# Finishing stage of a two-layer transformer taken into the coupling stage: turn back, residual, normalise and store, two tiles at a time, a thousand tokens behind

## The chip, the cores and the metric

The kernel runs on one core of a Trainium2 chip, as one launch. The metric is the device time of that core in microseconds (us). The kernel before took 5580.25 us, the median of three runs (5573.52 to 5586.86).

## What is computed

Two post-norm layers over 4096 tokens of 256 features, all in float32. Each layer is an attention block and a feed-forward block, and behind each block the residual is added and the row normalised. The change touches only the last block, the "coupling" network of the second layer, and the last normalisation. Cut to what matters:

```python
def _L1_ffn_ref(x, ...):
    gf = _global_net(x.mean(axis=1, keepdims=True), ...)      # one number for the sequence
    out = x
    for _ in range(3):
        # tf: 256 -> 256 -> 128 -> 64 -> 1 with gelu between, sigmoid at the end, one number per token
        tf = _coupling_net(out, cn_w1, cn_b1, ..., cn_w4, cn_b4)
        combined = 0.7 * gf + 0.3 * tf
        coupling = 0.1 + adaptive_range * (combined - 0.5) * 2.0
        out = out + coupling * _twist(out)                    # _twist swaps the halves with signs
    return out

x = _layernorm(x + _L1_ffn_ref(x, ...), axis=-1)              # the last line of the reference
```

So each token goes three times through a small network, which changes it; then its old value is added, its 256 features are normalised, and the row is stored.

## The kernel before

The kernel is a chain of stages: `project` and `attention` for layer 0, `mlp_weights` and `mlp`, `project` and `attention` for layer 1, `mix_out`, `coupling`, `finish`. Between two stages stand `core.clear()`, which frees the semaphores, and a barrier of all engines. Within a stage every engine has its own instruction stream, in the order in which the code is written, and waits on semaphores (`wait_ge`) that the others raise (`then_inc`). No scheduler moves anything.

Names: a tile is 128 tokens (P), there are 32 (NT). A block is 512 tokens (QB), there are 8 (N). `x_all` (in `build` it is `a_all`) holds the layer's input with tokens on partitions, `xT_all` the same values with features on partitions, in two chunks c of 128 features. `ps` is the accumulator memory with eight banks of 512 floats.

`coupling` works on pairs of blocks: a loop `r` over 4 pairs, in it 3 cycles `cyc`, in it both blocks `q` of the pair, layer by layer. TensorE computes layer 1 for both blocks (L1541, banks 2q and 2q+1), then layer 2 (L1549, bank 4+q), then layers 3 and 4 (L1554 and L1557, both in bank 6+q). ScalarE follows with gelu, gelu, gelu and tanh (L1578 and L1579, L1583, L1587, L1591). VectorE then makes the coefficient (L1506), two products (L1510, L1511), and changes `xT_all` in place (L1513, L1514); the last raises `x_new[q]`. In cycles 1 and 2 layer 1 of a block waits for `x_new[q]`; in cycle 0 it doesn't, since the next pair of blocks is independent of the last. TensorE, ScalarE and VectorE each run the loop with a hardware counter (`Fori`) and take addresses and wait values from registers. A float32 matmul stands in the trace as two MATMUL records.

`finish` then goes over the 32 tiles, one at a time. TensorE turns a tile of `xT_all` back with two transposes (L1610). VectorE adds the old value (L1640), takes the statistics (L1645, L1647), adds epsilon (L1649); GpSimd raises to the power -0.5 (L1622); VectorE normalises (L1631); SyncE's queue stores the tile (L1656). In VectorE's order the normalisation of tile i-1 stands behind the addition of tile i and ahead of its statistics.

## Time and profile before

| | |
|---|---|
| median of three runs | 5580.25 us (5573.52 to 5586.86) |
| the profiled execution's own time | 5566.02 us |
| its span | 5564.2 us |
| TensorE busy | 5047.7 us, 91% |
| VectorE busy | 4709.1 us, 85% |
| ScalarE busy | 3734.5 us, 67% |
| GpSimd busy | 218.6 us, 4% |

Most of the span is attention, in two stretches with all three compute engines busy. The two stages of this change are the last 292 us: `coupling` computes from 5272.0 us on, its last write is done at 5500.1 us, and `finish` takes the rest. Times are us from the start of the span. An entry "[3.16 <-DVE xT_all L1514]" says that the engine was idle for 3.16 us before the row and that this instruction ended it; "PE" is TensorE's matmuls, "PEld" its weight loads, DVE is VectorE, ACT ScalarE, POOL GpSimd, SP SyncE. A row with "xN" merges N instructions and its time runs from the start of the first to the end of the last. "PEclk" is the clock granted to TensorE, 1.00 for 2.4 GHz and 0.50 for 1.2 GHz.

### The profile page before, as it was taken

What the parts mean: (1) busy time and instruction counts of PE and PEld (TensorE: products, weight loads), DVE (VectorE), ACT (ScalarE), POOL (GpSimd) and SP (SyncE); (2) the same over time, 40 slices, a digit from 0 to 9 for tenths busy, and PEclk for the clock granted to TensorE, in tenths of its full rate; (3) what the DMA queues carried; (4) which work ended last, traced back from release to release, by engine and by line L of the source; (5) the groups of instructions that cost most, each with busy time, mean ns of one, the idle gap of its engine ahead of it and who ended that gap; (6) DMA issues with size and microseconds to landing.
All of it is one profiled execution on the core that took longest, in us unless ns stands there. A gap on an engine that the chain in (4) does not pass through costs nothing. (4 is left out here: it accounts for less than half of the span.)

```text
span 5564.2 us, 124831 instructions
## 1 busy us (share of the span) xinstructions
PE 5047.7 (91%) x43370; PEld 2092.7 (38%) x43370; DVE 4709.1 (85%) x5375; ACT 3734.5 (67%) x7102; POOL 218.6 (4%) x278
## 2 busy tenths in 40 slices
PE   7599999999999588767999999999999999999686
PEld 4233434433444255432333333333333333333332
DVE  3588889889888689739999999999999999999535
ACT  2068787787777311123888888888888888888331
POOL 3100000000000000030000000000000000000201
PEclk7589999999999799986999999999999999999886
DMA  4301010010010100060100001000100001000000
GB/s 125 102 18 31 14 35 15 11 41 8 11 41 11 27 11 12 17 204 12 41 8 5 5 18 31 5 5 8 38 8 8 5 5 41 8 5 5 8 0 30
DMA packets 152926, 142.93 MB, mean 26 GB/s; under 512 B 72490, under 2 KB 107242, under 8 KB 152298
## 3 DMA queue, kind: packets, MB, share of 16 engines
q1 hardware_dynamic: 152330, 134.93, 8.6%
q8 instruction: 380, 6.23, 0.5%
q14 instruction: 216, 1.77, 0.1%
HBM read 86.84 MB, written 46.66 MB: 24 GB/s over the span
## 5 line engine op out<-in xcount | busy, mean ns | idle before, releaser
L926 DVE TENSOR_REDUCE att_mx<-ps 128x2 f32<-128x1024 f32 (+2 forms) x3335 | 3899.7, 1193 | 284.9 <-PE ps L801 208.5
L907 ACT ACTIVATE att_probs<-ps 128x512 f32<-128x512 f32 (+3 forms) x6400 | 3388.7, 583 | 644.1 <-PE ps L843 202.0
L870 PE MATMUL ps<-att_probs,att_V 128*17 128x256 f32 (+1 forms) x25088 | 1950.0, 385 | 0.0
L843 PE MATMUL ps<-att_Q,K 50*128 50x512 f32 (+3 forms) x6400 | 1675.8, 491 | 44.6 <-ACT att_probs L907 24.8
L801 PE MATMUL ps<-K,att_Q 48*128 48x512 f32 x6670 | 1460.0, 419 | 140.2 <-DMA K<-khi_scratch 81.7
L843 PEld LDWEIGHTS ps<-att_Q,K 50*128 50x128 f32 x6400 | 649.9, 184 | 1383.1 <-ACT att_probs L907 1314.8
L870 PEld LDWEIGHTS ps<-att_probs,att_V 128*17 128x17 f32 x25088 | 426.7, 96 | 1054.5 <-issue 590.3
L801 PEld LDWEIGHTS ps<-K,att_Q 48*128 48x128 f32 x6670 | 668.2, 192 | 229.0 <-DVE att_mx L926 138.0
L887 ACT ACTIVATE att_negT<-ps 32x128 fp32r<-32x128 f32 x66 | 16.6, 252 | 231.9 <-PE ps L811 231.9
L1181 PE MATMUL ps<-wguT,mlp_xqT 128*128 128x512 f32 (+1 forms) x384 | 163.4, 577 | 0.5 <-DVE mlp_h L1284 0.2
L791 PE MATMUL ps<-att_band,att_pick 64*128 64x128 bf16 x2080 | 162.9, 224 | 0.0
L1506 DVE TENSOR_SCALAR cn_cf<-cn_th,cn_ab 128x512 f32<-128x512 f32 x24 | 13.0, 544 | 151.5 <-ACT cn_th L1591 151.5
L1541 PE MATMUL ps<-xT_all,cn_w 128*128 x192 | 109.9, 737 | 27.7 <-DVE xT_all L1514 25.8
L1220 ACT ACTIVATE mlp_gate<-ps 128x704 f32<-128x704 f32 x32 | 24.2, 758 | 144.3 <-PE ps L1181 139.4
L1226 ACT ACTIVATE mlp_hqT<-ps 128x640 f32<-128x640 f32 x32 | 22.5, 703 | 132.6 <-PE ps L1190 132.6
L483 DVE TENSOR_TENSOR proj_qprod<-ps,proj_tabT 128x1024 f32<-128x1024 f32 x32 | 38.4, 1220 | 82.0 <-PE ps L329 82.0
L1362 POOL MEMSET mix_power<- 128x1 f32 x1 | 0.1, 98 | 2697.8 <-POOLq L131 2697.8
L1181 PEld LDWEIGHTS ps<-wguT,mlp_xqT 128*128 128x128 f32 x384 | 74.4, 201 | 74.6 <-issue 66.2
L1199 PE MATMUL ps<-wdT,mlp_hqT 128*128 128x256 f32 (+1 forms) x384 | 95.3, 391 | 1.1 <-DVE mlp_y L1258 1.1
L392 ACT ACTIVATE proj_xT<-ps 128x512 f32<-128x512 f32 x32 | 17.5, 595 | 117.2 <-PE ps L311 117.2
L1578 ACT ACTIVATE cn_h<-ps,cn_b 128x512 f32<-128x512 f32 x24 | 16.5, 687 | 114.4 <-PE ps L1541 114.4
L791 PEld LDWEIGHTS ps<-att_band,att_pick 64*128 64x128 bf16 x2080 | 67.9, 96 | 50.6 <-issue 26.6
(211 smaller groups left out, 2424.6 us busy)
## 6 DMA issues: line engine op xcount, KB each, us to landing
K<-khi_scratch SPq DMA_DIRECT2D x320, 64.0 KB, 2.3
att_Q<-qhi_scratch SPq DMA_DIRECT2D x272, 64.0 KB, 2.3
att_V<-v_scratch SPq DMA_DIRECT2D x80, 136.0 KB, 2.5
K<-klo_scratch SPq DMA_DIRECT2D x160, 64.0 KB, 2.3
v_scratch<-proj_vpad SPq DMA_DIRECT2D x16, 544.0 KB, 3.4
att_Q<-qlo_scratch SPq DMA_DIRECT2D x136, 64.0 KB, 2.3
att_Q<-att_negT SPq DMA_DIRECT2D x264, 4.0 KB
proj_x<-in_L_attn_x SPq DMA_DIRECT2D x8, 512.0 KB, 5.4
```

Source lines behind the costliest of these rows:

```text
L483: dve.tensor_tensor(prod[name][:, m], of[name], tabT[:, j % 2, m, :].unsqueeze(1).to_broadcast([P, 2, B]), ALU.mult).then_inc(prods[name], 1)
L791: return pe.matmul(dst, pick[rows, m], band[rows, m, kind], start=False, stop=(m == 1))
L801: mm = pe.matmul(bank(b)[:, 0:wide], Q[rows, slot_of(u), j, qt * P:(qt + 1) * P], K[rows, u // NQB, j, c * QB:c * QB + wide], start=True, ...
L843: mm = pe.matmul(ring(at)[:, lo:QB], K[rows, u // NQB, j, kt * P:(kt + 1) * P], Q[rows, slot_of(u), j, lo:QB], start=True, stop=not diagonal)
L870: mm = pe.matmul(ps[VW * h:VW * h + HV, 6, lo:(part + 1) * (QB // 2)], V[:, v // NQB, kt, HV * h:HV * (h + 1)], probs[:, (n_key[v] + kt) % ...
L907: act.activation(probs[:, (n_key[u] + kt) % PBUFS, column(h), lo:QB], ring(at)[:, lo:QB], ACT.Exp, scale=SCALE).then_inc(emptied, 1)
L926: dve.tensor_reduce(mx[:, min(u % NQB, 1), :, j, qt, c], ps[:, 2 + 2 * pair:4 + 2 * pair, 0:max_width(u, i) // 2], AX.X, ALU.max).then_inc ...
L1181: mm = pe.matmul(gu_ps[:, b:to], xqT[:, par, c, :], wguT[:, c, b:to], start=(c == 0), stop=(c == DC - 1))
L1199: mm = pe.matmul(down, hqT[0:kw, par, k, :], wdT[0:kw, k, :], start=(k == 0), stop=(k == NK - 1))
L1220: act.activation(gate[:], gate_ps, ACT.Silu).then_inc(s["gate_kept"], 1)
L1226: act.activation(hqT[:, par, 0:full], hqT_ps[:, 0:full], ACT.Copy).then_inc(s["hq_kept"], 1)
L1541: mm = pe.matmul(ps[:, 2 * q + m, :], w1[:, c, m * P:(m + 1) * P], xT_all[:, c, bass.ds(r * (2 * QB) + q * QB, QB)], start=(c == 0), stop= ...
```

## The change

`finish` as a stage of its own is gone, with the clear and barrier before it. Its work is in `coupling`, on pairs of tiles (256 tokens, 16 pairs p, four to each r):

- TensorE turns pair p back with four transposes into bank 6 + p % 2. While loop r works on its 1024 tokens, the four pairs of r-1 are turned back, behind layer 1 of both blocks and ahead of layer 2: two pairs in cycle 0, one each in cycles 1 and 2. The last four pairs come after the loop.
- VectorE settles a pair (addition over 512 columns, two normalisations of the pair before, two of each statistics instruction, one epsilon) at four places, `hosts`: in cycle 0 behind block 0 and behind block 1, in cycles 1 and 2 behind block 1. The last four pairs, and the last normalisation, come after the loop.
- GpSimd takes one power per pair, SyncE stores one pair (256 KB) per DMA, 16 instead of 32.
- Banks 6 and 7 are given to the pairs, so layer 3 goes to bank 2q and layer 4 to bank 4+q. Layer 1 now also waits for the gelu that read layer 3 of the cycle before, layer 2 for the tanh of the cycle before.
- The loops over r are written out instead of counted by hardware, on all engines.

```diff
@@ -1408,7 +1408,7 @@
                         steps.end()
 
 
-def coupling(nc, core, ps, w, xT_all, sums):
+def coupling(nc, core, ps, ident, w, xT_all, sums, x_all, out):
 
 
     CYCLES = 3
@@ -1444,7 +1444,15 @@
         coef = core.pair("cn_coef")
         twisted = core.pair("cn_twisted")
         x_new = core.pair("cn_x_new")
+        y, z = sb("y", [P, 2, 2, D]), sb("z", [P, 2, 2, D])
+        st, mv = sb("st", [P, 2, 6]), sb("mv", [P, 2, 2, 2])
+        var, rstd, power = sb("var", [P, 2, 2]), sb("rstd", [P, 2, 2]), sb("power", [P, 2])
+        f = {n: core.sem("cn_" + n) for n in ("turned", "ln_steps", "root", "normed")}
+        stored = core.pair("cn_stored")
         NETS = 13
+        PAIR_STEPS = 6
+        PAIRS_R = 2 * QB // (2 * P)
+        hosts = {(0, 0): 0, (0, 1): 1, (1, 1): 2, (2, 1): 3}
         with nc.Block() as block:
             @block.sync
             def _(sp):
@@ -1460,6 +1468,12 @@
+                for p in range(NT // 2):
+                    sp.wait_ge(f["normed"], 2 * p + 2)
+                    sp.dma_start(out[2 * p * P:(2 * p + 2) * P, :].rearrange("(g p) d -> p g d", p=P), z[:, p % 2]
+                                 ).then_inc(stored[p % 2], 16)
+                for par in range(2):
+                    sp.wait_ge(stored[par], 16 * (NT // 4))
 
             @block.gpsimd
             def _(pool):
@@ -1468,6 +1482,14 @@
                 pool.memset(sign[P // 2:P], -1.0).then_inc(s["set"], 1)
+                pool.wait_ge(s["set"], 3)
+                pool.memset(power[:], -0.5).then_inc(s["set"], 1)
+                pool.wait_ge(s["set"], 4)
+                for p in range(NT // 2):
+                    pool.wait_ge(f["ln_steps"], (p + 1) * PAIR_STEPS)
+                    if p >= 2:
+                        pool.wait_ge(f["normed"], 2 * (p - 1))
+                    pool.tensor_tensor(rstd[:, p % 2], var[:, p % 2], power[:], ALU.pow).then_inc(f["root"], 1)
 
             @block.vector
             def _(dve):
@@ -1496,12 +1518,40 @@
 
                 for q in range(2):
                     dve.sem_inc(coef[q], 1)
-                with dve.Fori(0, N // 2) as r:
+
+                def norm(p):
+                    dve.wait_ge(f["root"], p + 1)
+                    if p >= 2:
+                        dve.wait_ge(stored[p % 2], 16 * (p // 2))
+                    for t in range(2):
+                        dve.tensor_scalar(z[:, p % 2, t], y[:, p % 2, t], mv[:, p % 2, t, 0:1], rstd[:, p % 2, t:t + 1],
+                                          ALU.subtract, ALU.mult).then_inc(f["normed"], 1)
+
+                def settle(p):
+                    steps = Chain(dve, f["ln_steps"], p, PAIR_STEPS)
+                    dve.wait_ge(f["turned"], p + 1)
+                    if p >= 2:
+                        dve.wait_ge(f["normed"], 2 * (p - 1))
+                    steps.put(dve.tensor_tensor(y[:, p % 2], ps[:, 6 + p % 2, :].rearrange("p (t d) -> p t d", t=2),
+                                                x_all[:, 2 * p:2 * p + 2, :], ALU.add))
+                    if p >= 1:
+                        norm(p - 1)
+                    steps.ready()
+                    for t in range(2):
+                        steps.put(dve.bn_stats(st[:, t], y[:, p % 2, t]))
+                    steps.ready()
+                    for t in range(2):
+                        steps.put(dve.bn_aggr(mv[:, p % 2, t], st[:, t]))
+                    steps.ready()
+                    steps.put(dve.tensor_scalar(var[:, p % 2], mv[:, p % 2, :, 1], EPS, None, ALU.add))
+                    steps.end()
+
+                for r in range(N // 2):
                     for cyc in range(CYCLES):
                         for q in range(2):
                             at = r * CYCLES + cyc
-                            a = xT_all[:, 0, bass.ds(r * (2 * QB) + q * QB, QB)]
-                            b = xT_all[:, 1, bass.ds(r * (2 * QB) + q * QB, QB)]
+                            a = xT_all[:, 0, (2 * r + q) * QB:(2 * r + q + 1) * QB]
+                            b = xT_all[:, 1, (2 * r + q) * QB:(2 * r + q + 1) * QB]
                             dve.wait_ge(act_done[3][q], at + 2)
                             dve.tensor_scalar(cf[:, q], th[:, q], ab[:, 4:5], ab[:, 5:6], ALU.mult, ALU.add
                                               ).then_inc(coef[q], 1)
@@ -1512,6 +1562,11 @@
                             dve.wait_ge(twisted[q], at + 1)
                             dve.tensor_tensor(a, a, turn[:, q, 0], ALU.add)
                             dve.tensor_tensor(b, b, turn[:, q, 1], ALU.subtract).then_inc(x_new[q], 1)
+                            if r >= 1 and (cyc, q) in hosts:
+                                settle((r - 1) * PAIRS_R + hosts[cyc, q])
+                for p in range(NT // 2 - PAIRS_R, NT // 2):
+                    settle(p)
+                norm(NT // 2 - 1)
 
             @block.tensor
             def _(pe):
@@ -1528,7 +1583,19 @@
                 for n in range(4):
                     for q in range(2):
                         pe.sem_inc(mm_done[n][q], 1)
-                with pe.Fori(0, N // 2) as r:
+
+                def turn_back(p):
+                    r, q = p // PAIRS_R, p % PAIRS_R // 2
+                    pe.wait_ge(x_new[q], (r + 1) * CYCLES)
+                    if p >= 2:
+                        pe.wait_ge(f["ln_steps"], (p - 2) * PAIR_STEPS + 1)
+                    for t in range(2):
+                        for c in range(DC):
+                            mm = pe.transpose(ps[:, 6 + p % 2, (t * DC + c) * P:(t * DC + c + 1) * P],
+                                              xT_all[:, c, (2 * p + t) * P:(2 * p + t + 1) * P], ident[:])
+                    mm.then_inc(f["turned"], 1)
+
+                for r in range(N // 2):
                     for cyc in range(CYCLES):
                         at = r * CYCLES + cyc
                         for q in range(2):
@@ -1536,25 +1603,31 @@
                             if cyc > 0:
                                 pe.wait_ge(x_new[q], at)
                             pe.wait_ge(act_done[0][q], at + 1)
+                            pe.wait_ge(act_done[2][q], at + 1)
                             for m in range(2):
                                 for c in range(DC):
                                     mm = pe.matmul(ps[:, 2 * q + m, :], w1[:, c, m * P:(m + 1) * P],
-                                                   xT_all[:, c, bass.ds(r * (2 * QB) + q * QB, QB)],
+                                                   xT_all[:, c, (2 * r + q) * QB:(2 * r + q + 1) * QB],
                                                    start=(c == 0), stop=(c == DC - 1))
                             mm.then_inc(mm_done[0][q], 1)
+                        if r >= 1:
+                            for p in ((0, 1), (2,), (3,))[cyc]:
+                                turn_back((r - 1) * PAIRS_R + p)
                         for q in range(2):
                             pe.wait_ge(act_done[0][q], at + 2)
                             pe.wait_ge(act_done[1][q], at + 1)
+                            pe.wait_ge(act_done[3][q], at + 1)
                             for c in range(DC):
                                 mm = pe.matmul(ps[:, 4 + q, :], w2[:, c, :], h1[:, q, c], start=(c == 0), stop=(c == DC - 1))
                             mm.then_inc(mm_done[1][q], 1)
                         for q in range(2):
                             pe.wait_ge(act_done[1][q], at + 2)
-                            pe.wait_ge(act_done[3][q], at + 1)
-                            pe.matmul(ps[0:H3, 6 + q, :], w3[:], h2[:, q], start=True, stop=True).then_inc(mm_done[2][q], 1)
+                            pe.matmul(ps[0:H3, 2 * q, :], w3[:], h2[:, q], start=True, stop=True).then_inc(mm_done[2][q], 1)
                         for q in range(2):
                             pe.wait_ge(act_done[2][q], at + 2)
-                            pe.matmul(ps[:, 6 + q, :], w4w[:], h3[:, q], start=True, stop=True).then_inc(mm_done[3][q], 1)
+                            pe.matmul(ps[:, 4 + q, :], w4w[:], h3[:, q], start=True, stop=True).then_inc(mm_done[3][q], 1)
+                for p in range(NT // 2 - PAIRS_R, NT // 2):
+                    turn_back(p)
 
             @block.scalar
             def _(act):
@@ -1569,7 +1642,7 @@
                 for n in range(4):
                     for q in range(2):
                         act.sem_inc(act_done[n][q], 1)
-                with act.Fori(0, N // 2) as r:
+                for r in range(N // 2):
                     for cyc in range(CYCLES):
                         at = r * CYCLES + cyc
                         for q in range(2):
@@ -1584,79 +1657,11 @@
                         for q in range(2):
                             act.wait_ge(mm_done[2][q], at + 2)
                             act.wait_ge(mm_done[3][q], at + 1)
-                            act.activation(h3[:, q], ps[0:H3, 6 + q, :], ACT.Gelu, bias=b3[:, 0:1]).then_inc(act_done[2][q], 1)
+                            act.activation(h3[:, q], ps[0:H3, 2 * q, :], ACT.Gelu, bias=b3[:, 0:1]).then_inc(act_done[2][q], 1)
                         for q in range(2):
                             act.wait_ge(mm_done[3][q], at + 2)
                             act.wait_ge(coef[q], at + 1)
-                            act.activation(th[:, q], ps[:, 6 + q, :], ACT.Tanh, bias=half_b[:, 0:1], scale=0.5).then_inc(act_done[3][q], 1)
-
-
-def finish(nc, core, ps, ident, x_all, xT_all, out):
...
@@ -1709,9 +1714,7 @@
...
-        coupling(nc, core, ps, nets, xT_all, sums)
-        core.clear()
-        finish(nc, core, ps, ident, a_all, xT_all, out)
+        coupling(nc, core, ps, ident, nets, xT_all, sums, a_all, out)
```

How this moves instructions, first on TensorE. The rows of the coupling loop before, whose body is three such cycles (`cn_w`, `cn_w4w` are the network's weights, `cn_h` its hidden values; a row counts a float32 matmul once):

```order
L1541 MATMUL ps<-xT_all,cn_w 128x512 x8
L1546 REGISTER_ALU
L1549 MATMUL ps<-cn_h,cn_w 128x512 x4
L1554 MATMUL ps<-cn_h,cn_w 64x512 x2
L1557 MATMUL ps<-cn_h,cn_w4w 128x512 x2
L1541 MATMUL ps<-xT_all,cn_w 128x512 x8
```

And in the changed kernel, cycles 0 and 1 of a later r (L1594 are the transposes, `ident` the unit matrix):

```order
L1609 MATMUL ps<-xT_all,cn_w 128x512 x8
L1594 MATMUL ps<-ident,xT_all 128x128 x8
L1621 MATMUL ps<-cn_h,cn_w 128x512 x4
L1625 MATMUL ps<-cn_h,cn_w 64x512 x2
L1628 MATMUL ps<-cn_h,cn_w4w 128x512 x2
L1609 MATMUL ps<-xT_all,cn_w 128x512 x8
L1594 MATMUL ps<-ident,xT_all 128x128 x4
```

Eight transposes stand between layers 1 and 2 in cycle 0, four in cycles 1 and 2; 48 of the 64 stand in the loop.

VectorE, cycle 0 of a later r in the changed kernel: block 0, the settling of a pair, block 1, the settling of the next (`cn_cf` is the coefficient, `cn_turn` the products, `cn_y` and `cn_z` a pair before and after normalising).

```order
L1556 TENSOR_SCALAR cn_cf<-cn_th,cn_ab 128x512
L1560 TENSOR_TENSOR cn_turn<-cn_cf,xT_all 128x512
L1561 TENSOR_TENSOR cn_turn<-cn_cf,xT_all 128x512
L1563 TENSOR_TENSOR xT_all<-xT_all,cn_turn 128x512
L1564 TENSOR_TENSOR xT_all<-xT_all,cn_turn 128x512
L1535 TENSOR_TENSOR cn_y<-ps,a_all 128x512
L1527 TENSOR_SCALAR cn_z<-cn_y,cn_mv,cn_rstd 128x256 x2
L1541 BN_STATS cn_st<-cn_y 128x6 x2
L1544 BN_AGGR cn_mv<-cn_st 128x2 x2
L1546 TENSOR_SCALAR cn_var<-cn_mv 128x2
L1556 TENSOR_SCALAR cn_cf<-cn_th,cn_ab 128x512
L1560 TENSOR_TENSOR cn_turn<-cn_cf,xT_all 128x512
```

Before, the five instructions of block 1 followed those of block 0 directly; now eight instructions of a pair stand between. On the same engine behind the loop, before:

```order
L1514 TENSOR_TENSOR xT_all<-xT_all,cn_turn 128x512
L1499 REGISTER_ALU
L1499 COMPARE_AND_BRANCH
L1448 UNCONDITIONAL_BRANCH
L1625 UNCONDITIONAL_BRANCH
L1640 TENSOR_TENSOR fin_y<-ps,a_all 128x256
L1645 BN_STATS fin_st<-fin_y 128x6
L1647 BN_AGGR fin_mv<-fin_st 128x2
L1649 TENSOR_SCALAR fin_var<-fin_mv 128x1
```

Now the last write of the loop is followed by the last hosted pair and, the same five rows each, the four pairs behind the loop:

```order
L1564 TENSOR_TENSOR xT_all<-xT_all,cn_turn 128x512
L1535 TENSOR_TENSOR cn_y<-ps,a_all 128x512
L1527 TENSOR_SCALAR cn_z<-cn_y,cn_mv,cn_rstd 128x256 x2
L1541 BN_STATS cn_st<-cn_y 128x6 x2
L1544 BN_AGGR cn_mv<-cn_st 128x2 x2
L1546 TENSOR_SCALAR cn_var<-cn_mv 128x2
L1535 TENSOR_TENSOR cn_y<-ps,a_all 128x512
```

So five pairs, not sixteen, are settled behind the last write to `xT_all`.

## Rows read from the trace of the kernel before

**Rows 1.** The page: the span, and TensorE's granted clock in 40 slices.

```profile
span 5564.2 us, 124831 instructions
...
PEclk7589999999999799986999999999999999999886
```

**Rows 2.** Busy time by stretch: each engine (instructions), PEclk, DMA share, GB/s.

```profile
5271.90:5500.15 228.25, 196.11 (x384) 75.10 (x384) 74.16 (x120) 79.70 (x120) 0.00 (x0) 0.86 0.00 0
5500.15:5564.20 64.05, 21.76 (x64) 9.39 (x64) 46.06 (x160) 0.00 (x0) 17.66 (x33) 0.50 0.19 66
...
5402.20:5412.00 9.80, 9.79 (x17) 4.29 (x18) 3.00 (x5) 1.37 (x3) 0.00 (x0) 0.74 0.00 0
...
2925.20:2926.00 0.80, 0.80 (x10) 0.63 (x8) 0.79 (x1) 0.50 (x2) 0.00 (x0) 1.00 0.00 0
```

**Rows 3.** Timeline, last cycle of coupling: start, length, instruction, idle before it.

```profile
5476.85 9.87 PE L1541 MATMUL ps<-xT_all,cn_w 128*128 x16 [3.16 <-DVE xT_all L1514]
...
5483.32 0.69 ACT L1578 ACTIVATE cn_h<-ps,cn_b 128x512 f32<-128x512 f32 x1 [8.91 <-PE ps L1541]
...
5487.41 0.19 PEld L1549 LDWEIGHTS ps<-cn_h,cn_w 128*128 128x128 f32 x1 [0.24 <-issue]
5488.07 0.39 PEld L1549 LDWEIGHTS ps<-cn_h,cn_w 128*128 128x128 f32 x2 [0.47 <-ACT cn_h L1579]
...
5493.10 0.69 ACT L1591 ACTIVATE cn_th<-ps,cn_half_b 128x512 f32<-128x512 f32 x1 [0.37 <-PE ps L1557]
```

**Rows 4.** Timeline, from cycle 0 to cycle 1 of the third pair of blocks.

```profile
5402.21 9.64 PE L1541 MATMUL ps<-xT_all,cn_w 128*128 x16 [3.28 <-DVE xT_all L1514]
...
5404.70 0.69 DVE L1514 TENSOR_TENSOR xT_all<-xT_all,cn_turn 128x512 f32 x1
5408.46 0.69 ACT L1578 ACTIVATE cn_h<-ps,cn_b 128x512 f32<-128x512 f32 x1 [8.81 <-PE ps L1541]
```

**Rows 5.** Timeline, transposes of 128x128: in attention, in projection, in finish.

```profile
2925.21 0.66 PE L879 MATMUL ps<-ident,att_outT 128*128 128x128 f32 x4
2925.79 0.50 PE L843 MATMUL ps<-att_Q,K 50*128 50x512 f32 x2
...
87.42 1.09 PE L311 MATMUL ps<-ident,proj_x 128*128 128x128 f32 x8 [0.50 <-DMA proj_x<-in_L_attn_x]
...
5501.05 1.09 PE L1610 MATMUL ps<-ident,xT_all 128*128 128x128 f32 x4 [7.13 <-PEq L131]
```

**Rows 6.** Timeline, coupling's last write and one tile of finish.

```profile
5499.46 0.68 DVE L1514 TENSOR_TENSOR xT_all<-xT_all,cn_turn 128x512 f32 x1
...
5504.77 0.15 DVE L1649 TENSOR_SCALAR fin_var<-fin_mv 128x1 f32<-128x1 f32 x1
...
5505.59 0.41 DVE L1631 TENSOR_SCALAR fin_z<-fin_y,fin_mv,fin_rstd 128x256 f32<-128x256 f32 x1 [0.31 <-POOL fin_rstd L1622]
5505.92 0.42 DVE L1645 BATCH_NORM_STATS2 fin_st<-fin_y 128x6 f32<-128x256 f32 x1
5506.38 0.18 DVE L1647 BATCH_NORM_AGGREGATE fin_mv<-fin_st 128x2 f32<-128x6 f32 x1
5506.59 0.15 DVE L1649 TENSOR_SCALAR fin_var<-fin_mv 128x1 f32<-128x1 f32 x1
5506.67 0.42 DVE L1640 TENSOR_TENSOR fin_y<-ps,a_all 128x256 f32<-128x256 f32 x1
...
5506.90 0.55 POOL L1622 TENSOR_TENSOR fin_rstd<-fin_var,fin_power 128x1 f32<-128x1 f32 x1 [1.35 <-DVE fin_var L1649]
5507.49 0.41 DVE L1631 TENSOR_SCALAR fin_z<-fin_y,fin_mv,fin_rstd 128x256 f32<-128x256 f32 x1 [0.39 <-POOL fin_rstd L1622]
```

**Rows 7.** Timeline, the last normalisation; DMA issues: count, KB each, us to landing.

```profile
5561.27 0.41 DVE L1631 TENSOR_SCALAR fin_z<-fin_y,fin_mv,fin_rstd 128x256 f32<-128x256 f32 x1 [0.66 <-POOL fin_rstd L1622]
...
out<-fin_z SPq DMA_DIRECT2D x32, 128.0 KB, 1.7
...
v_scratch<-proj_vpad SPq DMA_DIRECT2D x16, 544.0 KB, 3.4
```

59 lines of the change are left out of this document (1 added, 58 removed).

## The prediction

> **What bounds the kernel now.** I read the views in the order of the end of the program backwards. The page's clock line [rows 1] shows that only the last two of 40 slices and a few elsewhere are off the full clock; attention is untouched. The table by stretch [rows 2] gives the two stages: 228.25 us of coupling, where TensorE is busy 196.11 us and VectorE 74.16 us, and 64.05 us of finish, where VectorE is busy 46.06 us, TensorE 21.76 us and ScalarE not at all. So coupling is bound by TensorE with VectorE idle two thirds of the time, and finish by a chain through VectorE.
>
> The timeline of coupling shows one cycle [rows 3]: TensorE waits 3.16 us for the VectorE write of block 0, then runs without a stop until the last tanh can start. From layer 1's start at 5476.85 to the tanh at 5493.10 are 16.25 us, all on TensorE. The cycle is a loop: layer 1, 2, 3, 4, tanh, five VectorE instructions, layer 1 again. What is added to TensorE between layers 1 and 2 lengthens it one for one; what is added to VectorE lengthens it only if it delays a write that TensorE is waiting for.
>
> The timeline of finish [rows 6] shows a ring of one tile: from one normalisation (5505.59) to the next (5507.49) 1.90 us, the one before 1.82 by the same rows that stand between (var at 5504.77, normalisation at 5505.59). It goes normalise, statistics, aggregate, epsilon, power on GpSimd, normalise. 32 tiles of a mean 1.86 us are 59.4 us, which with the start and the last store make the 64.05 us.
>
> **What is removed: the stage of 64.05 us [rows 2].** All of it lies behind the last write to xT_all, which ends at 5499.46 + 0.68 = 5500.14 [rows 6]. I call that moment T.
>
> **What comes in its place: the tail behind T.** Five pairs are settled there, 11 to 15, since pair 11 is hosted behind the very last block. The ring for a pair, from [rows 6], with the distance between starts: first normalisation 0.33 (5505.59 to 5505.92), second 0.33, first statistics 0.34 (0.42 less the 0.08 by which a following instruction may overlap, as 5506.59 to 5506.67 shows against a length of 0.15), second 0.46 (it is waited for, 5505.92 to 5506.38), first aggregate 0.10 (0.18 less 0.08), second 0.21, then epsilon to the next normalisation 0.82 to 0.90, I take 0.86. The sum is 2.63 us per pair, against 3.71 for two single tiles. The addition over 512 columns (0.68 as the VectorE instruction of that width in [rows 6]) starts 0.08 behind epsilon and lets the next instruction start 0.61 later, at 0.69 of these 0.86 us, so GpSimd's power hides it. TensorE needs 1.09 us for four transposes at the low clock (5501.05, [rows 5]); each pair's bank is free two pairs ahead, so they are hidden by a ring of 2.63.
>
> The first normalisation (pair 10) starts at T - 0.07 + 0.61 = T + 0.54, that of pair 15 five rings later, T + 13.69, and its second half ends 0.33 + 0.41 later, T + 14.43. Before, the last normalisation ended at 5561.68 and the span at 5564.2, 2.52 us later, with a store of 128 KB that lands in 1.7 us [rows 7]. A store of 256 KB: the rows give 1.7 us for 128 KB and 3.4 for 544 KB, so 0.0 to 1.7 us more; on the line between them it is 0.5. The tail is 14.43 + 2.52 + 0.5 = 17.4 us. Bounds of the ring: below, the epsilon-to-normalise step at 0.82, 0.2 us in all; above, a pair at the pace of two tiles, 5 x (3.71 - 2.63) = +5.4.
>
> **What is added to TensorE in the loop.** 48 transposes: six groups of 4 (cycles 1 and 2, three times) and three of 8. In attention four transposes stand in a full stream and take 0.58 us from the first to the next matmul (2925.21 to 2925.79), at a clock of 1.00 [rows 2, 5]. Eight take, by projection's row, 1.09 - 0.27 for the last one's own length, plus one more step of 0.117: 0.94. The sum is 6 x 0.58 + 3 x 0.94 = 6.3 us. The places are behind at least ten matmuls of layer 1, where the clock is full again. One bubble goes: layer 2 of block 1 waits for the second gelu today, weight loads 0.66 apart instead of 0.43 (5487.41 to 5488.07, [rows 3]), and any transposes ahead of layer 2 cover these 0.23 us, nine times, 2.1. Net +4.2 us. Bounds: 48 x 0.117 less 2.1 is 3.5; at the low clock four transposes make a step of (1.09 - 0.42) / 3 = 0.22, 48 of them 10.6 with no bubble won.
>
> **What is added to VectorE in the loop.** Three of the four hosts stand behind block 1, where VectorE then waits for the next tanh: it is idle for (228.25 - 74.16) / 12 = 12.8 us per cycle [rows 2], and still some 8 ahead of a cycle 0, whose layer 1 runs at once and warm (3.2 us of hole and 3.0 of slow clock less). 2.5 us vanish there. The fourth stands between blocks 0 and 1 of cycle 0, and behind it are queued block 1's five instructions, for which TensorE's layer 1 of block 1 waits. Today block 1's write ends at 5405.39 [rows 4]. The pair costs 0.61 + 0.66 + 0.80 + 0.31 + 0.08 = 2.46 us, so it ends at 5407.85. TensorE starts layer 1 of block 0 at 5402.21; the gelu at 5408.46 shows its eighth record just ended, a record of 0.59 us, steps of 0.43, so block 1 could start at about 5408.1. The margin is 0.25 us: no cost, three times, up to 0.5 each if a pair costs as much as two single tiles on VectorE (+1.5). It holds only because TensorE runs this stretch at a mean clock of 0.74 [rows 2].
>
> **New waits.** Layer 1 waits for the gelu of layer 3 of the cycle before, which the same queue's layer 4 has already waited for; layer 2 for the last tanh, over several us before, since all of layer 1 lies between. The turn-back of the second pair in cycle 0 needs the addition of the pair hosted behind the last write of the r before; that write ends 7.0 us behind the start of the tanh of block 0 (5493.10 to 5500.14), the addition 0.7 later; TensorE starts the next layer 1 about 0.8 behind the same tanh, needs 16 x 0.43 = 6.9 us for it and 0.5 for the first pair, 8.2 against 7.7. Nil, with 0.5 us to spare. GpSimd's and SyncE's queues hold nothing else in this stage.
>
> **Loops written out.** Before cycle 1 TensorE's hole is 3.28 us, before cycle 2 3.16 [rows 3, 4]: register work on VectorE, 4 x 0.12 = 0.5 us, goes. The entry of the loops may give up to 1 us more, or nothing; I take 0.4.
>
> **Sum.** T moves by +4.2 - 0.5 - 0.4 = +3.3 us. The span becomes 5500.14 + 3.3 + 17.4 = 5520.8, 43.4 less than 5564.2. The profiled execution took 5566.02 us with that span, so its like would take 5522.6. The median shown, 5580.25, lies 14.2 above that execution; the parts before coupling are the same, so I forecast 5580.25 - 43.4 = 5536.8, rounded to 5537.
>
> **A rule weighed against this.** The clock is 1.00 in the 0.80 us that hold attention's four transposes, and it falls in coupling only behind holes of 3.2 us in which TensorE does nothing; behind them it is 0.74 over 9.8 us [rows 2]. The Trainium skill ("TensorE: Matmul & The Clock Gate", Part 4: PE-mode transpose) says that transposes don't count as busy time for the clock the way matmuls do. By that rule the up to eight transposes here could look like a hole; the trace has a group of four at the full clock, and none of eight in the midst of matmuls, so it speaks against it for four and is silent on eight. What it would cost is the third rival.
>
> **Rivals.**
> 1. The tail doesn't get the pair's discount (GpSimd's power on two columns, or the instructions' latency, is paid twice) and the transposes run at their upper bound: +5.4 and +6.4 us, 5549. For it: the ring is made of latencies that no row shows for pairs. Against: VectorE's work per tile is known and pipelined.
> 2. The hole disappears as a clock event: TensorE keeps 2.4 GHz over the holes. Layer 1's sixteen records take 9.87 us instead of 16 x 0.43 = 6.9, so eight holes would give back 8 x 3.0 = 24 us, while TensorE would wait for the hosted pair 2.2 us at three places: 5537 - 24 + 7 = 5520. Against: the holes stay as long as they are.
> 3. Slower: the transposes in the loop make the clock fall to 1.2 GHz for what follows in the cycle. Layers 2 to 4 are 16 records, which cost 0.43 us more each: 6.9 us, nine cycles, 62 us: 5599. It needs only a clock that stays low for 43.4 / 9 = 4.8 us' worth, eleven records of sixteen, to turn the gain into a loss. Against: the attention row.
> 4. The change doesn't hide the work because hosts and TensorE wait for each other (the margins above of 0.25 and 0.5 us): with a lost microsecond at each of nine places it is 5546, inside my range. To eat the gain it would need 4.8 us per cycle, for which no row speaks.
>
> **How the numbers follow.** A measurement of this kernel tells about 0.2% (11 us) from no change. Forecast with its own range of 5528 to 5547: 0.82. Rival 1: 0.07. Rival 2: 0.03. Rival 4: 0.03 (0.01 of it as a loss of the whole gain, within 0.2%). Rival 3: 0.05, of which 0.02 for a partial form that ends within 0.2%. Faster by over 0.2% is 0.94, within 0.03, slower 0.03. The bounds give 5537 - 0.7 - 0.2 - 0.5 - 0.6 = 5535 to 5537 + 6.4 + 5.4 + 1.5 + 1.2 + 0.9 = 5552; three runs of one kernel lie 13 us apart, so the low end is taken 11 below: 5524 to 5552.
>
> **What would show it.** Right: no row of a finish stage; about 17 us between the last xT_all write and the end; rings of 2.6 us; TensorE's cycle in the loop longer by 0.3 to 0.7 us; no idle of TensorE for block 1 in cycle 1; clock 1.00 over layers 2 to 4. Wrong: a clock below 1.00 behind the transposes, a wait of the transposes on VectorE, an idle VectorE between the pairs of the tail beyond the power, or a T more than 10 us late.

## The result, and the profile after

The changed kernel took 5518.73 us, the median of six runs (5514.80 to 5535.66), against 5576.89 us for six runs of the kernel before (5562.71 to 5586.86). The ratio is 0.9904, with a 95% interval of 0.9883 to 0.9925: faster by about 1%. Forecast were 5537 us and a range from 5524 to 5552, so the time lies 5 us below the range, and the medians moved by 58 us where 43 were forecast. The two profiled executions moved by 46.2 us (span 5564.2 to 5518.0).

First the stretches of the changed kernel, as in [rows 2] (columns as there). The first is coupling up to the last write to `xT_all`, the second everything behind it.

```profile
5272.50:5500.69 228.19, 197.59 (x436) 77.91 (x436) 99.19 (x209) 79.78 (x120) 8.29 (x11) 0.90 0.03 12
5500.69:5518.00 17.31, 3.26 (x12) 2.14 (x12) 12.72 (x42) 0.00 (x0) 3.49 (x5) 0.50 0.27 92
```

Coupling is as long as before, 228.2 us, with 52 matmul records and 25 us of VectorE work more in it, and at a mean clock of 0.90 instead of 0.86. What followed it took 64.05 us and takes 17.31.

The tail on VectorE, one pair of the four alike, with GpSimd's power, answers to [rows 6], and the last normalisation to [rows 7]:

```profile
5500.00 0.69 DVE L1564 TENSOR_TENSOR xT_all<-xT_all,cn_turn 128x512 f32<-128x512 f32 x1
5500.60 0.68 DVE L1535 TENSOR_TENSOR cn_y<-ps,a_all 128x512 f32<-128x512 f32 x1
5501.20 0.73 DVE L1527 TENSOR_SCALAR cn_z<-cn_y,cn_mv,cn_rstd 128x256 f32<-128x256 f32 x2
...
5503.89 0.74 DVE L1527 TENSOR_SCALAR cn_z<-cn_y,cn_mv,cn_rstd 128x256 f32<-128x256 f32 x2 [0.21 <-POOL cn_rstd L1492]
5504.54 0.75 DVE L1541 BATCH_NORM_STATS2 cn_st<-cn_y 128x6 f32<-128x256 f32 x2
5505.32 0.25 DVE L1544 BATCH_NORM_AGGREGATE cn_mv<-cn_st 128x2 f32<-128x6 f32 x2
5505.60 0.17 DVE L1546 TENSOR_SCALAR cn_var<-cn_mv 128x2 f32<-128x2 f32 x1
5505.69 0.69 DVE L1535 TENSOR_TENSOR cn_y<-ps,a_all 128x512 f32<-128x512 f32 x1
5505.85 0.70 POOL L1492 TENSOR_TENSOR cn_rstd<-cn_var,cn_power 128x2 f32<-128x2 f32 x1 [2.00 <-DVE cn_var L1546]
...
5506.59 0.73 DVE L1527 TENSOR_SCALAR cn_z<-cn_y,cn_mv,cn_rstd 128x256 f32<-128x256 f32 x2 [0.21 <-POOL cn_rstd L1492]
...
5514.66 0.74 DVE L1527 TENSOR_SCALAR cn_z<-cn_y,cn_mv,cn_rstd 128x256 f32<-128x256 f32 x2 [0.81 <-POOL cn_rstd L1492]
```

From normalisation to normalisation are 2.69 or 2.70 us. VectorE idles 0.21 us of it, for the power; the addition of the next pair fills the rest of that wait. Five such rings lead from 5501.20 to 5514.66, and the span ends 2.60 us after the last normalisation. A store of 256 KB lands in 2.1 us, by the DMA view of the last 120 us:

```profile
out<-cn_z SPq DMA_DIRECT2D x13, 256.0 KB, 2.1
```

In the loop, cycles 0 and 1 of the second r, with the transposes (L1594) between layers 1 (L1609) and 2 (L1621); they answer to [rows 4, 5]:

```profile
5329.56 7.13 PE L1609 MATMUL ps<-xT_all,cn_w 128*128 128x512 f32 x16
...
5336.53 1.04 PE L1594 MATMUL ps<-ident,xT_all 128*128 128x128 f32 x8
...
5337.40 3.60 PE L1621 MATMUL ps<-cn_h,cn_w 128*128 128x512 f32 x8
...
5347.92 8.83 PE L1609 MATMUL ps<-xT_all,cn_w 128*128 128x512 f32 x16 [3.15 <-DVE xT_all L1564]
...
5356.59 0.60 PE L1594 MATMUL ps<-ident,xT_all 128*128 128x128 f32 x4
...
5357.03 3.60 PE L1621 MATMUL ps<-cn_h,cn_w 128*128 128x512 f32 x8
```

Eight transposes set layer 2 back by 0.87 us, four by 0.44, and layer 2 keeps its 3.60 us. The hole ahead of cycle 1, in which TensorE waits for VectorE, is still there.

### The profile page after: what moved, and what is told of

Same layout as the page of the kernel before. It is cut to its first block and busy times, and to the rows that moved or that the text cites. A ratio compares the mean times of both kernels' runs of the same rounds, so it can differ in the third digit from the quotient of the medians.

```text
span 5518.0 us, 124529 instructions
## 1 busy us (share of the span) xinstructions
PE 5035.9 (91%) x43370; PEld 2086.1 (38%) x43370; DVE 4698.1 (85%) x5343; ACT 3736.7 (68%) x7102; POOL 213.0 (4%) x262
## 5 line engine op out<-in xcount | busy, mean ns | idle before, releaser
L1181 PE MATMUL ps<-wguT,mlp_xqT 128*128 128x512 f32 (+1 forms) x384 | 166.1, 584 | 0.3 <-DVE mlp_h L1284 0.2
L1609 PE MATMUL ps<-xT_all,cn_w 128*128 128x512 f32 x192 | 105.0, 707 | 27.1 <-DVE xT_all L1564 25.3
L1181 PEld LDWEIGHTS ps<-wguT,mlp_xqT 128*128 128x128 f32 x384 | 75.0, 203 | 76.4 <-issue 67.9
```

The lines of the kernel that those rows point to most:

```text
L1181: mm = pe.matmul(gu_ps[:, b:to], xqT[:, par, c, :], wguT[:, c, b:to], start=(c == 0), stop=(c == DC - 1))
L1609: mm = pe.matmul(ps[:, 2 * q + m, :], w1[:, c, m * P:(m + 1) * P], xT_all[:, c, (2 * r + q) * QB:(2 * r + q + 1) * QB], start=(c == 0), st ...
```

## The experiments

Theory A: the change acts only on the last two stages, where it is worth 46 to 47 us, and the other 12 us between the medians are scatter of single runs from stages that the change leaves alone. Theory B: something ahead of coupling got faster as well. Two further questions were the price of the transposes and what the holes do to the clock.

One caution holds for every stage length below. The first r (cycles 0 to 2 of the first pair of blocks) holds no transposes and no hosted pairs, yet its three layers 1 take different times from profile to profile: the very first one from 8.64 to 10.02 us in the eleven profiles in which TensorE does the same ahead of it. Lengths of whole stages therefore compare only to a microsecond or two. Where less is at stake I count from the start of the second r (its first layer 1) to the last write to `xT_all`: 170.28 us in the kernel before, 171.13 in the changed kernel.

**The kernel before, against itself.**

```diff
(no edit)
```

> The kernel before, unchanged, timed against itself. Theory A (the change acts only in the last two stages, and the rest of the 58 us between the medians is scatter of single runs): ratio 1.000 within 0.002, single runs 15 to 25 us apart, and stages ahead of coupling that differ by some us from one profiled execution to the next. Theory B (something ahead of coupling got faster by some 12 us): the same ratio, but single runs that stay as high as 5575 to 5587 us with little scatter, and coupling starting at 5272 us or later in every profile.

Ratio 0.999 (0.9975 to 1.0006), median 5571.38 us of 12 runs (5558.25 to 5581.98). The kernel before took 5573.27 us beside it, the median of 23 runs, 5552.70 to 5595.36: 43 us from the fastest to the slowest. The profiled execution of this unchanged kernel has a span of 5578.7 us, 14.5 us above that of [rows 1], and its last two stages are these:

```profile
5286.90:5514.70 227.80, 195.76 (x384) 74.74 (x384) 74.10 (x120) 79.77 (x120) 0.00 (x0) 0.86 0.00 0
5514.70:5578.70 64.00, 21.74 (x64) 9.39 (x64) 46.02 (x160) 0.00 (x0) 17.70 (x33) 0.50 0.19 66
```

They are the same to 0.5 us; coupling starts at 5286.9 instead of 5272.0 us. The whole difference of the two executions stands ahead of coupling. Where, the first and last starts of three transpose and matmul lines show: layer 1's maxima (L811, in both attentions), the gate and up matmuls of `mlp` (L1181), the turning in `mix_out` (L1329). The kernel before, then the same kernel again; the starts are the two numbers around "to":

```profile
L811 PE MATMUL ps<-ident,att_negp x66: 327/331/473, 302.1 to 5154.0; 128*128 128x128 f32 x66
...
L1181 PE MATMUL ps<-wguT,mlp_xqT x384: 485/593/1062, 1945.9 to 2318.1; 128*128 128x512 f32 x128, 128*128 128x384 f32 x64
...
L1329 PE MATMUL ps<-ident,b_all x64: 272/273/476, 5170.3 to 5242.7; 128*128 128x128 f32 x64
```

```profile
L811 PE MATMUL ps<-ident,att_negp x66: 327/331/477, 306.1 to 5168.9; 128*128 128x128 f32 x66
...
L1181 PE MATMUL ps<-wguT,mlp_xqT x384: 486/592/1131, 1957.6 to 2329.0; 128*128 128x512 f32 x128, 128*128 128x384 f32 x64
...
L1329 PE MATMUL ps<-ident,b_all x64: 272/273/477, 5185.3 to 5257.6; 128*128 128x128 f32 x64
```

4.0 us arise before the first attention's work, 7.7 between there and `mlp`, 3.3 between `mlp` and `mix_out`, where the second attention stands. That is as A expects.

**The changed kernel again.**

```diff
(no edit)
```

> The changed kernel, unchanged. A: the last write of coupling at about 5500.7 us, 17.3 us behind it to the end, median 46 us (40 to 52) below that of the kernel before, so a ratio near 0.9917. B: 55 to 60 us below, ratio 0.990 or less, and coupling starting 8 to 12 us earlier than in the kernel before.

Ratio 0.9909 (0.9890 to 0.9929), median 5527.12 us (5518.84 to 5530.65). Against the 5573.27 us beside it that is 46 us, as A expects, though the interval of the ratio takes in both theories. Its last two stages:

```profile
5279.10:5507.80 228.70, 198.09 (x436) 77.93 (x436) 99.19 (x208) 79.78 (x120) 8.29 (x11) 0.90 0.03 12
5507.80:5525.10 17.30, 3.26 (x12) 2.15 (x12) 12.66 (x42) 0.00 (x0) 3.48 (x5) 0.50 0.27 91
```

Coupling starts 7 us later than in the first profile of either kernel, not earlier; the two stages take 246.0 us (245.5 in the first), against 292.3 and 291.8 for the kernel before. That is 46 to 47 us in every pairing. From the start of the second r to the last write are 170.28 and 170.23 us in the two profiles of the kernel before, 171.13 and 171.21 in those of the changed kernel. No profile speaks for B: over all twelve of this study coupling starts between 5272.0 and 5289.3 us, in no order that follows the edits. The times alone don't exclude that B holds for a few microseconds: the two intervals of the ratio allow for 40 to 65 us.

**The loops written out, alone.** (`written_out`)

```diff
-                with dve.Fori(0, N // 2) as r:
+                for r in range(N // 2):
...
-                            a = xT_all[:, 0, bass.ds(r * (2 * QB) + q * QB, QB)]
+                            a = xT_all[:, 0, (2 * r + q) * QB:(2 * r + q + 1) * QB]
```

(and so on TensorE and ScalarE)

> The kernel before with the three loops over r written out and nothing else. A: coupling shorter by 0.5 us at the three holes ahead of a cycle 1 plus up to 1 us at the entry, the same finish, ratio 0.9997 to 1.000. B, if the written-out code is what speeds up the rest: ratio 0.998 or less.

Ratio 0.9987 (0.9971 to 1.0004): the interval holds A's 0.9997 and B's 0.998 alike. In the profile coupling starts at 5273.5 us, between the two of the kernel before, and takes 226.4 us instead of 228.2 and 227.8; finish takes 64.1 as before. Most of the 1.4 to 1.8 us is the first r, whose three layers 1 take 28.54 us instead of 29.82 and 29.54; they differ as much where no edit is near. From the second r on it is 170.07 us instead of 170.28 and 170.23. What the edit shows by itself is 0.12 us at each of four holes ahead of a cycle 1 (3.16 instead of 3.28), together 0.5 us, and ahead of the first layer 1, outside the stage as it is cut here, an idle of 1.50 us instead of 1.94 and 1.85. That is about 0.9 us.

**Each transpose of the loop four times.** (`turned_4x`)

```diff
+                    for again in range(4 if p < NT // 2 - PAIRS_R else 1):
                     for t in range(2):
                         for c in range(DC):
                             mm = pe.transpose(...)
```

> The changed kernel with each transpose of the loop issued four times (144 more; the last four pairs as before). If a transpose costs its step of 0.11 us on the chain, coupling is longer by 144 x 0.11 = 15.8 us. If transposes are read as idle time by the clock, the twelve or twenty-four extra ones ahead of layer 2 (1.8 to 3.5 us) let the clock fall, and layers 2 to 4 show records of 0.85 us step: 50 us or more. If the transposes had some cover, less than 10 us.

Coupling takes 247.1 us, 18.4 to 18.9 more. Cycle 0 of the second r:

```profile
5338.73 3.66 PE L1595 MATMUL ps<-ident,xT_all 128*128 128x128 f32 x32
5342.22 3.60 PE L1622 MATMUL ps<-cn_h,cn_w 128*128 128x512 f32 x8
```

32 transposes set layer 2 back by 3.49 us, 0.109 each, so 144 cost 15.7; the rest is layer 1, busy 108.2 us instead of 105.0, 1.0 of it in the first r, where the edit adds nothing. Layer 2 behind 3.5 us of nothing but transposes still takes 3.60 us, and the granted clock is 1.00 over both rows: no slower clock. That disposes of the third rival, in which transposes look idle to the clock.

**No transposes in the loop.** (`no_turns`)

```diff
+                for b in range(2):
+                    for t in range(4):
+                        pe.transpose(ps[:, 6 + b, t * P:(t + 1) * P], xT_all[:, 0, t * P:(t + 1) * P], ident[:])
...
+                    if p < NT // 2 - PAIRS_R:
+                        pe.sem_inc(f["turned"], 1)
+                        return
                     for t in range(2):
```

> The changed kernel without the 48 transposes of the loop: banks 6 and 7 are filled once ahead of it, and VectorE settles pairs 0 to 11 from what stands there, so these rows of the output are not the reference's. What the transposes cost the chain is the difference in coupling's length (228.2 and 228.7 us in two profiles of the changed kernel). By the prediction's term: shorter by 6.3 - 2.1 = 4.2 us, with the 0.23 us bubble back in all cycles. Rival (the transposes change when the clock comes back in layer 1, and that gives back what they cost): shorter by less than 1.5 us or longer, with layer 1 busy 108 to 110 us instead of 105.

This kernel leaves out the 48 transposes and keeps their waits. Coupling takes 224.09 us, 4.1 to 4.6 less. But most of that is the first r, in which neither kernel has a transpose: with the eight transposes of the filling directly ahead of it, its first layer 1 takes 7.75 us instead of 9.42, the next two 8.83 and 9.65 instead of 9.78 and 9.95. From the start of the second r on, where the transposes stand, it is 5504.79 - 5334.80 = 169.99 us, against 5500.69 - 5329.56 = 171.13 in the changed kernel and 171.21 in its second profile. So the 48 transposes cost 1.1 to 1.2 us in all. That meets the rival's "less than 1.5" and not the prediction's 4.2. The kernel before with its loops written out, which has neither transposes nor pairs in this stretch, takes as long as this one, 170.07 us.

Gross they cost 6 x 0.44 + 3 x 0.87 = 5.25 us: the second r's cycle 0 takes 17.50 us here, 18.36 with eight of them. Two things give back 4 us of it. The nine layers 1 from the second r on take 79.6 us here and 76.0 there (76.0 in the second profile too), 3.6 us. One of cycle 1 without transposes before it, to be held against the 8.83 above:

```profile
5352.30 9.58 PE L1615 MATMUL ps<-xT_all,cn_w 128*128 128x512 f32 x16 [3.16 <-DVE xT_all L1564]
```

The hole is the same, the slow part behind it is longer. The other 0.5 us is a wait that only this run has. In cycle 0 of the third and fourth r layer 2 starts late, here with the second r above it for comparison:

```profile
5334.80 7.13 PE L1615 MATMUL ps<-xT_all,cn_w 128*128 128x512 f32 x16
5341.77 3.60 PE L1627 MATMUL ps<-cn_h,cn_w 128*128 128x512 f32 x8
...
5389.22 7.13 PE L1615 MATMUL ps<-xT_all,cn_w 128*128 128x512 f32 x16
5396.35 3.67 PE L1627 MATMUL ps<-cn_h,cn_w 128*128 128x512 f32 x8
```

From the start of layer 1 to the end of layer 2 are 10.80 us instead of 10.57, 0.23 more, twice. The likely cause is the wait kept in `turn_back`, for the addition of the pair two before: in the third r that addition ends at 5396.10 us, layer 2 would be due at 5396.19, and the second r has no such wait. In the changed kernel the 0.44 us of the first pair's transposes cover it. It isn't the bubble of the prediction, which was to stand in all nine cycles: in the other seven layer 2 starts 0.16 or 0.17 us before layer 1's last record ends, as in the kernel before, and takes 3.60 us.

That the transposes shorten the slow part is no rule either. Four times as many (`turned_4x`) made the nine layers 1 longer than in the changed kernel, 78.2 us.

**Both pairs of cycle 0 behind block 1.** (`host_behind`)

```diff
-        hosts = {(0, 0): 0, (0, 1): 1, (1, 1): 2, (2, 1): 3}
+        hosts = {(0, 1): (0, 1), (1, 1): (2,), (2, 1): (3,)}
...
-                                settle((r - 1) * PAIRS_R + hosts[cyc, q])
+                                for p in hosts[cyc, q]:
+                                    settle((r - 1) * PAIRS_R + p)
```

> The changed kernel with both pairs of cycle 0 settled behind block 1, none between the blocks. If the pair between the blocks is within VectorE's margin: coupling the same within 0.5 us. If it makes TensorE wait in cycle 1 (0.4 us at the place where the gelu idles 2.53 instead of 2.17 us): up to 1 us shorter.

Coupling takes 229.3 us, 0.6 to 1.1 more than the changed kernel, and from the second r on 171.2, the same. In the changed kernel two of the later three layers 1 of cycle 1 take 9.20 us, the other 8.83. In both, block 1's first weight load waits for VectorE's write of block 1, 0.93 us behind the load before it where 0.24 is the rule:

```profile
5463.49 0.30 PEld L1609 LDWEIGHTS ps<-xT_all,cn_w 128*128 128x128 f32 x2 [0.93 <-DVE xT_all L1564]
```

The one without a wait is in the second r, where pair 0 stands between the blocks, with no pair before it to normalise. With both pairs behind block 1 all three take 8.83. That is 0.7 us won; the last layer 1 of the stage, 9.52 us instead of 8.83 with no edit near it, takes it back. VectorE wasn't late in the changed kernel: its write ends 5.44 us behind the start of layer 1, and the prediction had 5.64. TensorE was early, ready for block 1 after 5.2 us (8.83 less the 3.60 of block 1's eight records) instead of the 5.9 reckoned with, because the slow part of layer 1 is 0.8 us shorter than in the kernel before (8.83 against 9.64). That uses up the margin of 0.25 us and costs 0.37 us at each of two places.

**Matmuls in the hole.** (`fill_matmuls`)

```diff
+                            if cyc > 0 and q == 0:
+                                for again in range(3):
+                                    pe.matmul(ps[:, 1, :], w2[:, 0, :], w1[:].rearrange("p c e -> p (c e)"), start=True, stop=True)
                             if cyc > 0:
                                 pe.wait_ge(x_new[q], at)
```

> As host_behind, and TensorE issues three float32 matmuls of 512 columns (six records, 2.6 us, into bank 1, never read) behind layer 4, in the hole of 3.16 us ahead of cycles 1 and 2. If the hole is what drops the clock: layer 1 at a step of 0.43 throughout, busy about 85 to 90 us instead of 105, coupling shorter by 20 to 24 us, time below the changed kernel's by as much. If the clock falls in spite of the fill, or the fill is late for the hole: coupling the same or up to 3 us longer.

Ratio to the kernel before 0.9867 (0.9843 to 0.9891), median 5504.33 us. Coupling takes 210.6 us at a mean clock of 0.98:

```profile
5282.20:5492.80 210.60, 202.33 (x484) 80.45 (x484) 99.48 (x208) 79.77 (x120) 7.68 (x11) 0.98 0.04 13
```

Layer 1 is busy 87.5 us instead of 105.0, and TensorE idles 0.38 us ahead of it instead of 3.16. The gain is 18 us and not the 20 to 24 expected. The eight layers 1 behind holes take 74.3 us in the changed kernel, and at the 7.13 us that a cycle 0 takes they would be 57.0, so 17.3 was all that there was to win. All eight take 7.13 here.

**Transposes in the hole.** (`fill_turns`)

```diff
-                                for again in range(3):
-                                    pe.matmul(ps[:, 1, :], w2[:, 0, :], ...)
+                                for again in range(24):
+                                    pe.transpose(ps[:, 1, (again % 4) * P:(again % 4 + 1) * P], w1[:, 0, 0:P], ident[:])
```

> As fill_matmuls, with 24 transposes of 128x128 (2.6 us) in place of the three matmuls. If transposes don't count as work for the clock (the Trainium skill, TensorE: Matmul & The Clock Gate, Part 4): layer 1 busy 105 to 110 us as without a fill, coupling 228 us. If they do: the same 205 us as with matmuls.

The same as with matmuls (211.4 us against 210.6; the 205 in the expectation was too much for either). The first hole, filled with 24 transposes, and layer 1 behind it; then the stage:

```profile
5306.32 2.84 PE L1606 MATMUL ps<-ident,cn_w 128*128 128x128 f32 x24
5309.55 7.13 PE L1613 MATMUL ps<-xT_all,cn_w 128*128 128x512 f32 x16 [0.39 <-DVE xT_all L1564]
```

```profile
5289.30:5500.70 211.40, 203.15 (x628) 93.06 (x628) 99.45 (x208) 79.77 (x120) 7.68 (x11) 0.98 0.04 13
```

Layer 1 takes 7.13 us behind every hole, which is the time of a cycle 0. From 5307 to 5317 us the granted clock is 1.00. The one difference of 0.8 us to the matmuls is the first layer 1 of the stage, 9.89 us instead of 9.05. The Trainium skill ("TensorE: Matmul & The Clock Gate", Part 4) has transposes not counting as busy time the way matmuls do; here float32 transposes of 128x128 hold the clock exactly as matmuls do, and the measurement decides.

**Four pairs behind the last write.** (`four_behind`)

```diff
-        hosts = {(0, 1): (0, 1), (1, 1): (2,), (2, 1): (3,)}
+        hosts = {(0, 1): (0, 1), (1, 1): (2, 3)}
...
-                            for p in ((0, 1), (2,), (3,))[cyc]:
+                            for p in ((0, 1), (2, 3), ())[cyc]:
```

> As host_behind, with pair 3 of the r before turned back and settled in cycle 1 too, so that four pairs, not five, are left behind the last write. If the tail is a ring of 2.69 us per pair: 17.31 - 2.69 = 14.6 us behind the last write. If the first of the five was hidden by what the last block does anyway: 16 to 17.3 us.

14.60 us behind the last write instead of 17.31, which is one ring less:

```profile
5500.50:5515.10 14.60, 2.17 (x8) 1.43 (x8) 10.29 (x34) 0.00 (x0) 2.79 (x4) 0.50 0.26 90
```

So the first of the five was not hidden. Coupling takes 225.6 us, 3.7 less than in `host_behind`, with layer 1 busy 102.6 us instead of 106.2. Most of that is again the first r; from the second r on it is 170.2 us instead of 171.2.

**The turn-backs in the hole.** (`in_hole`)

```diff
-                        if r >= 1:
-                            for p in ((0, 1), (2, 3), ())[cyc]:
-                                turn_back((r - 1) * PAIRS_R + p)
...
                             pe.matmul(ps[:, 4 + q, :], w4w[:], h3[:, q], start=True, stop=True).then_inc(mm_done[3][q], 1)
+                        if cyc < 2:
+                            if r >= 1:
+                                for p in (2 * cyc, 2 * cyc + 1):
+                                    turn_back((r - 1) * PAIRS_R + p)
+                            for again in range(3 if r == 0 else 2):
+                                pe.matmul(ps[:, 1, :], w2[:, 0, :], ..., start=True, stop=True)
```

> As four_behind, with the transposes of the loop moved behind layer 4 of cycles 0 and 1, where TensorE waits for VectorE, and the hole filled up with two float32 matmuls (three where r is 0). By the reading so far the transposes are then free and the clock stays full: coupling 210.6 us (fill_matmuls) less 5.3 for the transposes plus 2.1 for the bubble of 0.23 us in nine cycles, 207 us, tail 14.6, ratio to the kernel before 0.985 or less. Rival (turn-backs ahead of layer 1 hold it up, or the clock falls): coupling 213 us or more.

Ratio 0.9878 (0.9849 to 0.9907), median 5503.83 us. By the profile the two stages take 206.1 + 14.7 = 220.8 us:

```profile
5289.20:5495.30 206.10, 198.11 (x476) 78.95 (x476) 102.11 (x217) 79.69 (x120) 8.36 (x12) 0.98 0.04 15
5495.30:5510.00 14.70, 2.17 (x8) 1.43 (x8) 10.34 (x35) 0.00 (x0) 2.78 (x4) 0.50 0.26 89
```

That is 25 us less than the changed kernel and 71 less than the kernel before. The expected 207 us for coupling were built on the returning bubble of 2.1 us, which doesn't exist; without it 205.3 would be due, and the first layer 1, 9.87 us instead of 9.05, is the rest. The expected ratio of 0.985 or less was missed: 71 us of 5568.84 make 0.987. Timing can't rank this version against the one with filled holes alone (their intervals overlap almost wholly), the profiles do: 227.9 there, 220.8 here. The tail gives 2.6 of it and the loop from the second r on 5.3 (159.4 and 154.0 us, the transposes now free), less the 0.8 of the first layer 1. Both beat the kernel before by their intervals; over the changed kernel the gain rests on the stage times and on medians 20 us below the 5524.4 of its twelve runs, which were not taken beside them.

## Why the prediction was right or wrong

The main terms (the stage that goes, the tail that comes) were right. The stated time was not, and neither was the account of TensorE in the loop. Point by point:

- **The removed stage.** 64.05 us were named, and they are gone.
- **The tail.** 17.4 us forecast, 17.31 measured. The ring is 2.69 us, not 2.63: power on two columns takes 0.70 us where one column took 0.55. The larger store ends 0.08 us later than the small one did (2.60 against 2.52), where 0.5 was allowed: its landing takes 2.1 instead of 1.7 us, but the time behind the last normalisation hardly grows. The first costs 0.3 us over five rings, the second gives 0.4 back: that the sum fits to 0.1 us is luck.
- **The transposes.** +4.2 us forecast, +1.1 to 1.2 measured (`no_turns`, from the second r on). The term had two mistakes of opposite sign and lacked a third part. The steps are shorter in this stream, 5.25 us in all instead of 6.3 (0.44 for four, not 0.58, a row of a place where TensorE's weight loads also waited for ScalarE). The bubble of 2.1 us was none: the gap in [rows 3] is between weight loads, which run ahead of the matmuls, while the eight matmul records take 3.60 us, 7 steps of 0.43 and one length of 0.59, with no gap in them. The row of the kernel before:

```profile
5486.55 3.60 PE L1549 MATMUL ps<-cn_h,cn_w 128*128 128x512 f32 x8
```

- **The slow part of layer 1.** The prediction had no term for it: it took the clock's recovery behind a hole as fixed. Against the kernel without transposes it got shorter by 3.6 us over nine cycles, and it depends on what went before in a way that no run here explains.
- **The loops.** -0.9 us forecast, and about 0.9 measured: 0.5 at four holes, the rest at the entry.
- **The pair between the blocks.** No cost forecast, with 0.25 us to spare; 0.37 us at two places of three measured. The prediction said that the margin rests on the slow clock of this stretch, 0.74 over 9.8 us, and over the 9.8 us behind the same start it is 0.83 in the changed kernel.
- **The sum.** T was to move by +3.3 us against the start of coupling; it moved by 0.0 (0.5 in the second profile), and from the second r on by 0.8 to 0.9. The span was forecast at 5520.8 us and was 5518.0.
- **The step that failed: "The median shown, 5580.25, lies 14.2 above that execution; the parts before coupling are the same, so I forecast 5580.25 - 43.4".** The parts are the same in code, but not in time: coupling starts anywhere within 17 us, and single runs of the kernel before spread over 43. Three runs fix the median no better than that; twelve runs of the kernel before in the timing against itself gave 5571.38, the 23 beside them 5573.27. The low end was set 11 us below the bound of 5535, for scatter of the measurement, as if the base were known. With the base at 5573.3 and the same 43.4 us the forecast would have been 5530. Of the 18 us between 5536.8 and 5518.7, 7 are this base and 3 the change itself, forecast at 43.4 and 46.2 in the profile. The remaining 8 stand in neither profile; what is left for them is the scatter of a median of six runs. The twelve runs of the changed kernel have a median of 5524.4 us (between 5521.75 and 5527.04), 48.9 below 5573.3; 46 to 47 of these are in the profiles. By that median the time would lie just inside the range, so missing it by 5 us is partly chance.
- **The rivals.** The dearer tail and transposes: no. A kept clock: not by this change. Filling the holes gave 18 us. The 24 were too many even for the kernel before, where the eight layers 1 behind holes take 78.6 us and would take 57.0 at 7.13 each, so 21.5; the 7 us of waits that were set against them were not measured, since the run that fills the holes has no pair between the blocks. A clock that falls behind transposes: refuted by 32 in a row. Waits between hosts and TensorE: 0.7 us.

What stays open: why the stages ahead of coupling differ by 15 us between executions of one program, why the first r does by 1 to 3, and what in the order of the work decides how long TensorE stays slow behind a hole. For the first two no experiment was made; as to the third, layers 1 behind equal holes of 3.16 us took from 8.83 to 10.19 us, and all I can say is that these times changed with edits elsewhere in the cycle.

## What to carry to other kernels

A stage that is bound by a chain of short instructions can cost little once it stands where the same engines idle: here 46 us of 64 went, for a loop longer by about 1 us and five pairs that come last. Look at the holes of the bounding engine before placing added work: what was put in the hole was free here, and it also kept the clock up, which was worth another 18 us. To price a small term, cut the stretch so that it holds only what the edit touches; 4.1 us of a whole stage were 1.1 us of the edit. Forecast a difference between stages from the trace, but take the absolute time from as many runs as there are, and give the base its own width.

## What the runs showed of the hardware that was not expected

- Float32 transposes of 128x128 keep TensorE at 2.4 GHz as matmuls do: 2.6 us of them in a hole, and 3.5 us of them between matmuls, with layer 1 at 7.13 and layer 2 at 3.60 us behind them.
- A hole of 0.4 us leaves the clock alone; holes of 3.15 to 3.29 us dropped it in every unfilled profile (0.56 over the 6 us from 5402.0 in the kernel before), and the layer behind took 8.83 to 10.19 us instead of 7.13, with values that repeat to 0.01 us (8.83, 9.20) where the cycle repeats.
- A gap between weight loads need not be one between matmuls: 0.66 us between two loads, and the eight matmul records around them without a gap.
